# Graph attention on one core: 17 tiles of gathered rows in place of 10 fetched row by row from two DMA queues

## The chip, the core and the metric

One core of a Trainium2 chip. The metric is the device time of one execution in microseconds (us), lower is better; this document gives medians of several executions, and reads one profiled execution instruction by instruction. The engines are TensorE (PE), VectorE (DVE), ScalarE (ACT), GpSimd (POOL) and SyncE (SP). "SPq" and "ACTq" in the rows are the instruction streams of SyncE and ScalarE that issue DMAs.

## What is computed

A graph attention layer with 6250 nodes, 100000 edges sorted by target node, 96 features and 8 heads, then a residual and a layer norm. Cut to what matters:

```python
Q_h = (x @ Wq + bq); K_h = (x @ Wk + bk); V_h = (x @ Wv + bv)      # 6250 x 96
E   = edge_attr @ We + be                                          # 100000 x 96
score = K_h[src] * Q_h[dst] / sqrt(12) * E                         # per edge
score = exp(clip(score.sum over the 12 features of a head, -5, 5))
msg   = V_h[src] * score
h_out = segment_sum(msg, dst) / (segment_sum(score, dst) + 1e-6)
out   = layernorm(x + h_out)
```

## The kernel before

**Tables.** The node projections are made first (lines 444 to 460 on PE, copies on ACT), and written to two tables in device memory: `kv_table` (a row of 192 floats for each node, its K and V) and `q_table`. Then the edges are worked through.

**Groups.** Edges come in 99 groups, numbered `at` = 0 to 98: 96 of 8 tiles of 128 edges and three small ones (8, 4 and 2 tiles). For every group:

- POOL gathers the rows K and V of the edges' source nodes out of `kv_table` into `kv`, one indirect DMA for each tile (L424). For the first four groups it gathers rows of `x` instead (L422), and PE projects them. The buffer `kv` holds U = 8 groups, so group `at` waits for `msg_done` of group `at - 8`. From group CLOSE = 16 on, POOL also waits at the start of group `at` until `q_done` is at least `at - 1` (L410), which is when PE has finished the query product (L516) of group `at - 2`.
- SP loads, four groups ahead of the query product, the edge features (`ea`, L248), windows of the queries (`qwin`, L259) and the relative targets (`rel_table` into `q_parts`, L243). Iteration `at` of its loop waits for `q_done` of group `at` (L356). Every fourth iteration reads 8 window starts from memory into registers (`window_rows`, L253).
- PE, in its iteration `at`: if `at` is a multiple of 4, it turns the finished block of sums (L537); then it turns the edge products of group `at + 1` into rows (L527), multiplies the edge features of group `at + 2` (L506) and selects the queries of group `at + 2` (L516); last come the sums of group `at` (L576).
- DVE, in its iteration `at`: `qke` (L955, waits for the gather of the group), `qe` of group `at + 1` (L872), the sum over heads `logit` (L964), `clipped` (L970), `place` (L860), then the weights and `msg` (L979, L982), then the comparison `pick` for group `at + 3` (L851). Between these stand the steps 0 to 11 of the layer norm of the block before, at fixed places (`BLOCK_PLACES`): steps 0 to 4 in groups with `at % 4 == 0`, steps 5 and 6 with 1, steps 7 to 11 with 2. Step 7 (L908) waits for ACT.
- ACT, in its iteration `at`: if `at % 4 == 0` the copy `accT` of the sums (L684); the exponential of group `at` (L690); the copy of the edge product of group `at + 2` into `qe` (L676); for some groups the copy described next (L701); the single-row loads described next; and if `at % 4 == 1` the two steps of the layer norm's root, `spread` (L663, L665).

**Tiles by row.** In ten groups (`BY_ROW`) POOL leaves out the last of the 8 tiles. Its 128 rows are fetched one by one: `load_single_rows` reads source nodes from memory into registers (TENSOR_LOAD, L216) and issues one DMA of 768 bytes for each (L220) into `kv_rows`, which lies in the memory of `q_full` and so appears under that name in the rows. SP does this for five of the tiles, 8 rows in every iteration from 4 on, ACT for the other five, 8 rows in every iteration from 4 on. When a tile's 128 rows have landed, ACT copies it into `kv` (L701) in the iteration before its group.

All engines take their instructions in program order, so an activation that stands behind DMA issues in ACT's stream waits until they are issued. The order is written out by hand.

Of the kernel before, what the change touches and what calls it, by code (L numbers as in the profile page):

```python
# [4 lines left out]
P = 128  # L5
N = 6250
# [5 lines left out]
T = 8  # L12
# [5 lines left out]
NR = (NW + 1) * P  # L18
# [2 lines left out]
EPS_LN = 1e-5  # L21
U = 8
CLOSE = 2 * U
SP_ROWS, ACT_ROWS = 8, 8
SP_TURNS, ACT_TURNS = -(-P // SP_ROWS), -(-P // ACT_ROWS)
FROM = 4
SP_TILES = tuple(22 + SP_TURNS * i for i in range(5))
ACT_TILES = tuple(23 + ACT_TURNS * i for i in range(5))
BY_ROW = SP_TILES + ACT_TILES
XG = 4  # L30
TURNS = NB // U
KV_CHUNKS = (4, 6, 10, 10, 8, 6, 4, 2)
# [2 lines left out]
QB = 5  # L35
QW = 42
# [24 lines left out]
def lap(r, k, ring):  # L61

    return (U // ring) * r + k // ring + 1


def gnn_program(nc, xT, xrows, src, src_row, dst_group, dst_tile, eaT, w_node, w_edge, out):
    f32, bf16, i32 = mybir.dt.float32, mybir.dt.bfloat16, mybir.dt.int32
    ALU, ACT, AX = mybir.AluOpType, mybir.ActivationFunctionType, mybir.AxisListType

    kv_table = nc.dram_tensor("kv_table", (NR, 2 * D), f32, kind="Internal").ap()  # L70
# [6 lines left out]
    with ctx:  # L77
        def sb(name, shape, dt):
            return ctx.enter_context(nc.sbuf_tensor(name, shape, dt))
# [24 lines left out]
        identity = sb("identity", [P, P], f32)  # L104
        xg = sb("xg", [P, XG, T, D], f32)

# [13 lines left out]
        qbase_int = sb("qbase_int", [P, 2 * NG], i32)  # L120
# [9 lines left out]

        idx = sb("idx", [P, NG * T], i32)
        ea = sb("ea", [DA, EAR, GE], f32)
        row_id = sb("row_id", [1, len(BY_ROW) * P], i32)
        kv_rows = q_full[:].rearrange("p t d -> p (t d)").rearrange("p (i f) -> p i f", f=2 * D)[:, 0:len(BY_ROW)]
        qwin = sb("qwin", [P, QRING, 2, D], bf16)
        place = sb("place", [P, 2, T, PW], f32)
# [32 lines left out]
        q_full_up, q_hi, q_r, q_mid, q_up = sem("q_full_up"), sem("q_hi"), sem("q_r"), sem("q_mid"), sem("q_up")  # L169
# [4 lines left out]
        idx_in, idx_rest_in = sem("idx_in"), sem("idx_rest_in")  # L174
        xg_in = [sem(f"xg_in{i}") for i in range(XG)]
        turned, turned_up, conv_mm, conv_up = sem("turned"), sem("turned_up"), sem("conv_mm"), sem("conv_up")
        row_id_in, rows_up = sem("row_id_in"), sem("rows_up")
        rows_in = [sem(f"rows_in{i}") for i in range(len(BY_ROW))]
        kv_in = [sem(f"kv_in{i}") for i in range(U)]
# [28 lines left out]
        def alone(at, t):  # L208

            return at in BY_ROW and t == T - 1  # L210

        def load_single_rows(eng, i, j, rows):

            count = min(rows, P - j * rows)
            edge = i * P + j * rows
            nodes = nc.values_load_multi_w_load_instructions(  # L216
                row_id[0:1, edge:edge + count], engines=[eng.engine], min_val=0, max_val=N - 1,
                skip_runtime_bounds_check_because="source nodes of edges are nodes")[1]
            for p in range(count):
                eng.dma_start(kv_rows[j * rows + p:j * rows + p + 1, i], kv_table[bass.ds(nodes[p], 1), :]  # L220
                              ).then_inc(rows_in[i], 16)

        def engine_turns(eng, body, unrolled):
# [15 lines left out]
        def edge_pass(first):  # L239
# [11 lines left out]
            def window_rows(sp, g, count):  # L251

                return nc.values_load_multi_w_load_instructions(  # L253
                    qbase_int[0:1, bass.ds(2 * g, 2 * count)], engines=[sp.engine], min_val=0, max_val=NR - QW)[1]

            def load_windows(sp, slot, bases):

# [5 lines left out]
            with nc.Block() as block:  # L263

                @block.sync
                def _(sp):
                    if first:
                        sp.dma_start(idx[:, 0:XG * T], src[:, 0:XG * T]).then_inc(idx_in, 16)
                        sp.dma_start(wn[:], w_node).then_inc(w_in, 16)
# [19 lines left out]
                        for c in range(5, len(KV_CHUNKS)):  # L289
# [3 lines left out]
                                     ranges[:, 0:4].rearrange("g (m h) -> g m h", m=2)).then_inc(range_out, 16)  # L293
                        sp.dma_start(idx[:, XG * T:], src[:, XG * T:]).then_inc(idx_rest_in, 16)
                        sp.wait_ge(range_out, 16)
# [54 lines left out]
                    def loads(r, k, at):  # L350


                        if at >= NG:
                            return
                        g, j, q, half = U * r + k, at % BG, U // BG * r + k // BG, k // BG % 2
                        sp.wait_ge(q_done, g + 1)  # L356
                        sp.sem_inc(loads_begun, 1)
                        if j == 0 and at + QRING < NG:
                            ahead[:] = window_rows(sp, g + QRING, min(BG, NG - at - QRING))
                        if at + QRING < NG:  # L360
                            load_windows(sp, k % QRING, ahead[2 * j:2 * j + 2])
                        if at + EAR < NG:
                            load_ea(sp, g + EAR, k % EAR)
                        if at + RELR < NG:
                            load_rel(sp, g + RELR, k % RELR)
                        if not first:
                            return
                        if j == 0 and at < NB:
                            if at >= 2 * BG:
                                sp.wait_ge(block_steps, BLOCK_STEPS * q - 2 * BLOCK_STEPS + 4)  # L370
                                sp.sem_inc(stores_begun, 1)
                            load_rows(q, half)
                        if j == 1 and at >= 2 * BG:
                            store_rows(q - 2, half, at)
                        turn = at - FROM
                        if turn == 0:
                            sp.wait_ge(row_id_in, 16)
                            sp.wait_ge(kv_out, 16 * len(KV_CHUNKS))
                        if 0 <= turn < len(SP_TILES) * SP_TURNS:
                            load_single_rows(sp, turn // SP_TURNS, turn % SP_TURNS, SP_ROWS)  # L380

                    engine_turns(sp, loads, first)
                    if first:
# [14 lines left out]
                def _(pool):  # L398
# [6 lines left out]
                    def gathers(at):  # L405
# [5 lines left out]
                        if first and at == 0:  # L411
                            pool.wait_ge(idx_in, 16)
                        if first and at == XG:
                            pool.wait_ge(idx_rest_in, 16)
                            pool.wait_ge(kv_out, 16 * len(KV_CHUNKS))
                        k = at % U
                        for t in range(tiles(at)):
                            if first and alone(at, t):
                                continue
                            sources = bass.IndirectOffsetOnAxis(ap=idx[:, at * T + t:at * T + t + 1], axis=0)  # L420
                            if first and at < XG:
                                pool.indirect_dma_start(xg[:, k, t], None, xrows, sources).then_inc(xg_in[k], 16)  # L422
# [6 lines left out]
                    for s in range(U):  # L429
                        groups = len(range(s, NG, U)) - (1 if first and s < XG else 0)  # L430
                        missing = (T - TAIL_TILES[s]) if s < len(TAIL_TILES) else 0
                        missing += sum(1 for at in BY_ROW if first and at % U == s)
                        pool.wait_ge(kv_in[s], 16 * (T * groups - missing))
# [160 lines left out]
                def _(act):  # L594
# [84 lines left out]
                    def weights(r, k, at):  # L679

                        g = U * r + k
                        if first and BG <= at < NG and at % BG == 0:
                            act.wait_ge(sum_done, g)
                            nc.scalar.activation(accT[:, 1 - k // BG], psA[0:ML, 0:BW], ACT.Copy).then_inc(block_up, 1)  # L684
                        if at < NG:
                            act.wait_ge(clip_done, g + 1)
                            nt = tiles(at)
                            if at >= 2:
                                act.wait_ge(sum_done, g - 1)
                            nc.scalar.activation(msg[:, k % 2, 0:nt, D:ML],  # L690
                                                 clipped[:, k % 2, 0:nt * H].rearrange("p (t h) -> p t h", t=nt),
                                                 ACT.Exp).then_inc(wt_done, 1)


                        if at + 2 < NG:
                            edges_up(r, k + 2, at + 2)
                        if first and at + 1 in BY_ROW:
                            i = BY_ROW.index(at + 1)
                            act.wait_ge(rows_in[i], 16 * P)
                            act.wait_ge(msg_done, at + 1 - U + 1)  # L700
                            nc.scalar.activation(kv[:, (at + 1) % U, T - 1], kv_rows[:, i], ACT.Copy).then_inc(rows_up, 1)  # L701
                        turn = at - FROM
                        if first and turn == 0:
                            act.wait_ge(row_id_in, 16)
                            act.wait_ge(q_up, NR // P // QB)
                        if first and 0 <= turn < len(ACT_TILES) * ACT_TURNS:
                            load_single_rows(act, len(SP_TILES) + turn // ACT_TURNS, turn % ACT_TURNS, ACT_ROWS)
                        if first and BG <= at < NG and at % BG == 1:
                            block_rstd(U // BG * r + k // BG - 1, BC)
                    edges_up(0, 0, 0)  # L710
# [406 lines left out]
```

## Time and profile before

| | |
|---|---|
| median of 3 runs | 995.9 us (994.56 to 996.25) |
| profiled execution, its own time | 993.86 us |
| its span in the trace | 992.1 us |
| busy share of the span: POOL, DVE, PE, ACT | 74%, 66%, 65%, 19% |
| mean granted TensorE clock | 0.807 of full speed |
| indirect DMAs on POOL | 32 (L422) and 740 (L424) |
| single-row DMAs | 640 on SP, 640 on ACT |

The time of an execution lies about 1.8 us over its span. Busy time does not count the issuing of DMAs on SP and ACT, register work or waits: an engine with a low share can still have a full instruction stream. For POOL the gathers count as busy while their descriptors are made, and the short piece of time between two of them is put down to "issue".

### The profile page before, as it was taken

How to read it: one execution, taken by the hardware profiler on the slowest of the kernel's cores; microseconds unless marked ns; L12 is line 12 of the kernel's file. 1: busy time of each engine (PE TensorE's matmuls, PEld its weight loads, DVE VectorE, ACT ScalarE, POOL GpSimd, SP SyncE). 2: the span in 40 equal slices, each digit the busy share in tenths (PEclk: the TensorE clock that was granted, in tenths of full speed). 3: DMA queues.
4: the chain of work that ended last, by engine and by line, in shares of the span. 5: the costliest groups of instructions: out<-in, count | busy, mean ns of one | idle time of the engine just before them, and what ended most of it. 6: DMA issues, size and time to landing. Idle time of an engine off the chain costs nothing. (4 is left out here: it accounts for less than half of the span.)

```text
span 992.1 us, 15976 instructions
## 1 busy us (share of the span) xinstructions
PE 643.3 (65%) x3276; PEld 419.8 (42%) x3276; DVE 653.0 (66%) x1307; ACT 189.4 (19%) x378; POOL 737.3 (74%) x778
## 2 busy tenths in 40 slices
PE   6778777766566766666557656664675566657563
PEld 5655555444343434344334434443343344334342
DVE  6638987877666675766566656664775566657655
ACT  4842211111111111111111111111111111111111
POOL 7777777777777777777777777777777777777772
PEclk9888988788877777778777877788788878777876
DMA  6999776666655557656565665565665655664531
GB/s 201 311 285 241 185 188 184 188 173 172 176 147 168 150 140 185 165 138 175 143 173 150 164 177 149 139 177 145 168 170 145 180 147 137 177 176 123 145 80 47
DMA packets 103482, 165.77 MB, mean 167 GB/s; under 512 B 46285, under 2 KB 66126, under 8 KB 103375
## 3 DMA queue, kind: packets, MB, share of 16 engines
q1 hardware_dynamic: 64399, 84.88, 31.3%
q0 software_dynamic: 36544, 74.37, 28.4%
q10 hardware_dynamic: 2432, 5.41, 1.6%
q14 instruction: 79, 0.65, 0.2%
q8 instruction: 28, 0.46, 0.2%
HBM read 152.19 MB, written 12.39 MB: 166 GB/s over the span
## 5 line engine op out<-in xcount | busy, mean ns | idle before, releaser
L424 POOL DMA_INDIRECT kv<-kv_table,idx x740 | 703.7, 951 | 225.6 <-issue 224.3
L527 PE MATMUL psT<-identity,qe 96*128 96x96 f32 x782 | 115.3, 307 | 242.7 <-DVE qe L872 242.6
L955 DVE TENSOR_TENSOR qke<-psT,kv 128x768 f32<-128x768 f32 (+1 forms) x99 | 93.6, 945 | 266.5 <-DMA kv<-kv_table,idx 257.2
L506 PE MATMUL psE<-ea,we 97*96 97x512 f32 x392 | 259.7, 799 | 0.8 <-ACT kv L646 0.8
L527 PEld LDWEIGHTS psT<-identity,qe 96*128 96x128 f32 x782 | 93.2, 178 | 259.8 <-DVE qe L872 259.7
L576 PE MATMUL psA<-place,msg 128*104 128x104 f32 x1536 | 170.1, 266 | 22.4 <-DVE msg L982 22.1
L576 PEld LDWEIGHTS psA<-place,msg 128*104 128x104 f32 x1536 | 160.1, 180 | 51.2 <-DVE msg L982 45.0
L676 ACT ACTIVATE qe<-psE 96x1024 f32<-96x1024 f32 (+1 forms) x99 | 99.8, 1008 | 217.2 <-PE psE L506 217.2
L872 DVE TENSOR_TENSOR qe<-psQ,qe 96x1024 f32<-96x1024 f32 (+1 forms) x99 | 118.4, 1196 | 7.8 <-ACT qe L676 7.8
L506 PEld LDWEIGHTS psE<-ea,we 97*96 97x96 f32 x392 | 75.9, 219 | 80.2 <-issue 80.2
L690 ACT ACTIVATE msg<-clipped 128x64 f32<-128x64 f32 (+1 forms) x99 | 25.3, 255 | 419.8 <-DVE clipped L970 413.8
L860 DVE TENSOR_TENSOR place<-psI,rel_tile 128x832 f32<-128x832 f32 (+1 forms) x99 | 98.3, 993 | 0.0
L982 DVE TENSOR_TENSOR msg<-kv,psI 128x768 f32<-128x768 f32 (+1 forms) x99 | 93.4, 943 | 3.4
L964 DVE TENSOR_REDUCE logit<-qke 128x64 f32<-128x768 f32 (+1 forms) x99 | 91.4, 923 | 0.0
L516 PE MATMUL psQ<-q_parts,qwin 126*96 126x512 bf16 x196 | 70.6, 446 | 0.8 <-DVE q_parts L851 0.8
L516 PEld LDWEIGHTS psQ<-q_parts,qwin 126*96 126x96 bf16 x196 | 30.0, 153 | 83.2 <-issue 81.4
L851 DVE TENSOR_SCALAR q_parts<-q_parts,query_id 126x1024 bf16<-126x1024 bf16 x99 | 50.6, 511 | 14.7 <-DMA q_parts<-rel_table 14.7
L537 PE MATMUL psA<-identity,accT 104*128 104x104 f32 x73 | 15.8, 331 | 52.5 <-ACT accT L684 52.1
L422 POOL DMA_INDIRECT xg<-xrows,idx x32 | 33.1, 1034 | 11.1 <-issue 9.4
L537 PEld LDWEIGHTS psA<-identity,accT 104*128 104x128 f32 x73 | 10.5, 206 | 56.8 <-ACT accT L684 56.2
L970 DVE TENSOR_SCALAR clipped<-logit 128x64 f32<-128x64 f32 (+1 forms) x99 | 22.7, 230 | 4.4
L684 ACT ACTIVATE accT<-psA 104x384 f32<-104x384 f32 x24 | 11.8, 490 | 69.8 <-issue 63.3
(105 smaller groups left out, 349.5 us busy)
## 6 DMA issues: line engine op xcount, KB each, us to landing
ea<-eaT SPq DMA_DIRECT2D x99, 384.0 KB, 4.0
q_parts<-rel_table SPq DMA_DIRECT2D x99, 252.0 KB
kv<-kv_table,idx POOLq DMA_INDIRECT x740
q_full<-kv_table SPq DMA_DIRECT2D x640, 0.8 KB
q_full<-kv_table ACTq DMA_DIRECT2D x640, 0.8 KB
qwin<-q_table SPq DMA_DIRECT2D x198, 23.6 KB
xb<-xrows SPq DMA_DIRECT2D x24, 144.0 KB
out<-ob SPq DMA_DIRECT2D x24, 144.0 KB
```

The lines of the kernel that those rows point to most:

```text
L424: pool.indirect_dma_start(kv[:, k, t], None, kv_table, sources).then_inc(kv_in[k], 16)
L506: last = nc.tensor.matmul(psE[0:D, h, 0:size], we[:], ea[:, k % EAR, edge:edge + size], start=True, stop=True)
L516: last = nc.tensor.matmul(psQ[0:D, h, 0:size], qwin[0:QR, k % QRING, h], pick[0:QR, k % 2, h * GE // 2:h * GE // 2 + size], start=True, st ...
L527: last = nc.tensor.transpose(psT[:, t % 2, t // 2 * D:(t // 2 + 1) * D], qe[0:D, k % 2, t * P:(t + 1) * P], identity[0:D, 0:D])
L576: last = nc.tensor.matmul(sums[0:ML, off:off + PW], msg[:, s, t], place[:, s, t], start=opens, stop=closes)
L676: nc.scalar.activation(qe[0:D, k % 2, 0:edges], psE[0:D].rearrange("d b e -> d (b e)")[:, 0:edges], ACT.Copy).then_inc(e_up, 1)
L851: nc.vector.tensor_scalar(pick[0:QR, k % 2], rel[0:QR, k % RELR], query_id[0:QR], None, ALU.is_equal).then_inc(pick_done, 1)
L860: nc.vector.tensor_tensor(place[:, k % 2, 0:nt], ps_ids.unsqueeze(1).broadcast_to([P, nt, PW]), rel_tile[:, bass.ds(g * T, nt)].unsqueeze( ...
L872: nc.vector.tensor_tensor(qe[0:D, k % 2, 0:edges], psQ[0:D].rearrange("d b e -> d (b e)")[:, 0:edges], qe[0:D, k % 2, 0:edges], ALU.mult). ...
L955: nc.vector.tensor_tensor(qke[:, 0:nt].rearrange("p (t b) d -> p b t d", **by_bank), psT[:, :, 0:nt // 2 * D].rearrange("p b (t d) -> p b ...
L964: nc.vector.tensor_reduce(logit[:, 0:nt * H], qke[:, 0:nt].rearrange("p t (h d) -> p (t h) d", h=H), AX.X, ALU.add).then_inc(logit_done, 1)
L982: nc.vector.tensor_tensor(msg[:, s, 0:nt, 0:D].rearrange("p t (h d) -> p t h d", h=H), kv[:, k, 0:nt, D:2 * D].rearrange("p t (h d) -> p t ...
```

## The change

Seven more groups have a tile fetched by rows. ACT now fetches eleven tiles (groups 13, 21, ... 93), 16 rows in each iteration from 4 to 91, in two portions of 8: the first behind the exponential and ahead of the copy of `qe`, the second where the portion stood before. SP fetches six tiles (groups 18, 31, ... 83), 10 rows in each iteration from 4 to 81, in portions of 8 and 2. Each portion has its own read of source nodes from memory, and the host lays the node numbers out so that each portion begins at a multiple of 8. The eight window starts that SP reads in every fourth iteration are no longer asserted to lie in range.

```diff
-SP_ROWS, ACT_ROWS = 8, 8
+SP_ROWS, ACT_ROWS = 10, 16
+SP_STEP, ACT_STEP = 8, 8
 SP_TURNS, ACT_TURNS = -(-P // SP_ROWS), -(-P // ACT_ROWS)
 FROM = 4
-SP_TILES = tuple(22 + SP_TURNS * i for i in range(5))
-ACT_TILES = tuple(23 + ACT_TURNS * i for i in range(5))
+SP_TILES = tuple(18 + SP_TURNS * i for i in range(6))
+ACT_TILES = tuple(13 + ACT_TURNS * i for i in range(11))
...
-        def load_single_rows(eng, i, j, rows):
-
-            count = min(rows, P - j * rows)
-            edge = i * P + j * rows
+        def load_single_rows(eng, i, turn, rows, begin, end):
+
+            start = turn * rows + begin
+            count = min(turn * rows + end, P) - start
+            if count <= 0:
+                return
+            edge = row_slot(i, turn, rows, begin)
...
-                    qbase_int[0:1, bass.ds(2 * g, 2 * count)], engines=[sp.engine], min_val=0, max_val=NR - QW)[1]
+                    qbase_int[0:1, bass.ds(2 * g, 2 * count)], engines=[sp.engine], min_val=0, max_val=NR - QW,
+                    skip_runtime_bounds_check_because="the lowest target node of half a group, at most N")[1]
...
-                            load_single_rows(sp, turn // SP_TURNS, turn % SP_TURNS, SP_ROWS)
+                            for begin in range(0, SP_ROWS, SP_STEP):
+                                load_single_rows(sp, turn // SP_TURNS, turn % SP_TURNS, SP_ROWS, begin,
+                                                 min(SP_ROWS, begin + SP_STEP))
...
+                        turn = at - FROM
+                        rows_due = first and 0 <= turn < len(ACT_TILES) * ACT_TURNS
+                        if rows_due and turn == 0:
+                            act.wait_ge(row_id_in, 16)
+                            act.wait_ge(q_up, NR // P // QB)
+                        if rows_due:
+                            load_single_rows(act, len(SP_TILES) + turn // ACT_TURNS, turn % ACT_TURNS, ACT_ROWS,
+                                             0, ACT_STEP)
                         if at + 2 < NG:
                             edges_up(r, k + 2, at + 2)
...
-                        turn = at - FROM
-                        if first and turn == 0:
-                            act.wait_ge(row_id_in, 16)
-                            act.wait_ge(q_up, NR // P // QB)
-                        if first and 0 <= turn < len(ACT_TILES) * ACT_TURNS:
-                            load_single_rows(act, len(SP_TILES) + turn // ACT_TURNS, turn % ACT_TURNS, ACT_ROWS)
+                        if rows_due:
+                            load_single_rows(act, len(SP_TILES) + turn // ACT_TURNS, turn % ACT_TURNS, ACT_ROWS,
+                                             ACT_STEP, ACT_ROWS)
                         if first and BG <= at < NG and at % BG == 1:
                             block_rstd(U // BG * r + k // BG - 1, BC)
```

ACT's stream before, in iteration 5 and up to the exponential of iteration 6 (a pair "ISA, DMA" is one row fetched, and there are 8 pairs):

```order
L690 ACTIVATE msg<-clipped 128x8x8
L676 ACTIVATE qe<-psE 96x1024
L216 TENSOR_LOAD row_id
L220 ISA
L220 DMA q_full<-kv_table 1x192
...
L663 ACTIVATE spread<-spread 128x3
L665 ACTIVATE spread<-spread 128x3
L690 ACTIVATE msg<-clipped 128x8x8
```

The same stretch of ACT's stream after the change (lines have other numbers: 705 for 690, 691 for 676, 228 and 232 for 216 and 220, 678 and 680 for 663 and 665; there are 8 pairs in each portion):

```order
L705 ACTIVATE msg<-clipped 128x8x8
L228 TENSOR_LOAD row_id
L232 ISA
L232 DMA q_full<-kv_table 1x192
...
L691 ACTIVATE qe<-psE 96x1024
L228 TENSOR_LOAD row_id
L232 ISA
L232 DMA q_full<-kv_table 1x192
...
L678 ACTIVATE spread<-spread 128x3
L680 ACTIVATE spread<-spread 128x3
L705 ACTIVATE msg<-clipped 128x8x8
```

A read of node numbers and eight row DMAs now stand between the exponential and the copy of `qe`, and a second set stands where the first stood, ahead of `spread` and the next exponential.

SP's stream after the change, one iteration (two window loads, edge features, relative targets, then portions of 8 and of 2 rows; before, the second TENSOR_LOAD of `row_id` and two of the row DMAs were not there):

```order
L272 DMA qwin<-q_table 126x96
L260 DMA ea<-eaT 96x1024
L255 DMA q_parts<-rel_table 126x1024
L228 TENSOR_LOAD row_id
...
L228 TENSOR_LOAD row_id
L232 ISA
L232 DMA q_full<-kv_table 1x192
L232 ISA
L232 DMA q_full<-kv_table 1x192
L272 ISA
```

One TENSOR_LOAD and two pairs have come into SP's iteration. In every fourth iteration `window_rows` held one TENSOR_LOAD and 16 ISA instructions; now it is the TENSOR_LOAD alone.

POOL's stream, the gathers of groups, before and after in one piece of the difference:

```order
-L422 DMA xg<-xrows,idx 128x96 x32
-L424 DMA kv<-kv_table,idx 128x192 x740
+L437 DMA xg<-xrows,idx 128x96 x32
+L439 DMA kv<-kv_table,idx 128x192 x733
```

Seven gathers are gone.

## Rows read from the trace of the kernel before

**Rows 1.** Head of the page: span, busy time by engine.

```profile
span 992.1 us, 15976 instructions
PE 643.3 (65%) x3276; PEld 419.8 (42%) x3276; DVE 653.0 (66%) x1307; ACT 189.4 (19%) x378; POOL 737.3 (74%) x778
```

**Rows 2.** Groups: line, engine, operation, count | busy us, mean ns | idle before, releasers.

```profile
L424 POOL DMA_INDIRECT kv<-kv_table,idx x740 | 703.7, 951 | 225.6 <-issue 224.3 <-PE psQ L516 0.6 <-DVE msg L982 0.6
```

**Rows 3.** Timeline of POOL: start us, us, instruction [idle before <-releaser].

```profile
2.85 1.09 POOL L422 DMA_INDIRECT xg<-xrows,idx  x1 [1.70 <-DMA idx<-src]
...
165.52 0.95 POOL L424 DMA_INDIRECT kv<-kv_table,idx  x1 [0.30 <-issue]
166.77 0.94 POOL L424 DMA_INDIRECT kv<-kv_table,idx  x1 [0.30 <-issue]
...
973.73 0.95 POOL L424 DMA_INDIRECT kv<-kv_table,idx  x1 [0.30 <-issue]
```

**Rows 4.** Waits, whole span: total us, times, longest us.

```profile
DVE qke L955 <- DMA kv<-kv_table,idx: 257.2, 71, 7.9
ACT accT L684 <- issue: 63.3, 20, 3.5
ACT spread L663 <- issue: 62.8, 20, 3.4
DVE spread L908 <- ACT spread L665: 9.1, 6, 2.3
```

**Rows 5.** Groups (as in rows 2): the product that DVE makes from the `qe` copy.

```profile
L872 DVE TENSOR_TENSOR qe<-psQ,qe 96x1024 f32<-96x1024 f32 (+1 forms) x99 | 118.4, 1196 | 7.8 <-ACT qe L676 7.8
```

**Rows 6.** Timeline of ACT, iterations 4 to 12 in part, and 92.

```profile
100.50 0.26 ACT L690 ACTIVATE msg<-clipped 128x64 f32<-128x64 f32 x1 [1.29 <-DVE clipped L970]
...
109.86 3.29 ACTq L220 DMA_DIRECT2D q_full<-kv_table  x8
113.20 0.21 ACT L663 ACTIVATE spread<-spread 128x3 f32<-128x3 f32 x1 [3.21 <-issue]
113.44 0.21 ACT L665 ACTIVATE spread<-spread 128x3 f32<-128x3 f32 x1
115.26 0.26 ACT L690 ACTIVATE msg<-clipped 128x64 f32<-128x64 f32 x1 [1.62 <-DVE clipped L970]
...
127.44 0.49 ACT L684 ACTIVATE accT<-psA 104x384 f32<-104x384 f32 x1 [3.13 <-issue]
129.13 0.26 ACT L690 ACTIVATE msg<-clipped 128x64 f32<-128x64 f32 x1 [1.20 <-DVE clipped L970]
133.51 1.02 ACT L676 ACTIVATE qe<-psE 96x1024 f32<-96x1024 f32 x1 [4.12 <-PE psE L506]
134.39 3.20 ACTq L220 DMA_DIRECT2D q_full<-kv_table  x8
137.69 0.26 ACT L690 ACTIVATE msg<-clipped 128x64 f32<-128x64 f32 x1 [3.17 <-DVE clipped L970]
...
159.27 0.49 ACT L684 ACTIVATE accT<-psA 104x384 f32<-104x384 f32 x1 [3.12 <-issue]
160.77 0.26 ACT L690 ACTIVATE msg<-clipped 128x64 f32<-128x64 f32 x1 [1.01 <-DVE clipped L970]
...
933.21 0.26 ACT L690 ACTIVATE msg<-clipped 128x64 f32<-128x64 f32 x1 [6.90 <-DVE clipped L970]
```

**Rows 7.** Timeline of PE, the query product of group 14.

```profile
162.63 0.60 PE L516 MATMUL psQ<-q_parts,qwin 126*96 126x512 bf16 x2
```

**Rows 8.** Line L220 on ACT's queue: ns min/median/max.

```profile
L220 ACTq DMA_DIRECT2D q_full<-kv_table x640: 234/235/547, 103.2 to 849.3; - x160
```

**Rows 9.** Timeline of SP's stream, end of iteration 15, start of 16.

```profile
178.57 3.16 SPq L220 DMA_DIRECT2D q_full<-kv_table  x8
184.83 0.86 SPq L259 DMA_DIRECT2D qwin<-q_table  x2
```

More of the change, by code:

```diff
@@ L23 @@
 CLOSE = 2 * U
-SP_ROWS, ACT_ROWS = 8, 8
+SP_ROWS, ACT_ROWS = 10, 16
+SP_STEP, ACT_STEP = 8, 8
 SP_TURNS, ACT_TURNS = -(-P // SP_ROWS), -(-P // ACT_ROWS)
 FROM = 4
-SP_TILES = tuple(22 + SP_TURNS * i for i in range(5))
-ACT_TILES = tuple(23 + ACT_TURNS * i for i in range(5))
+SP_TILES = tuple(18 + SP_TURNS * i for i in range(6))
+ACT_TILES = tuple(13 + ACT_TURNS * i for i in range(11))
 BY_ROW = SP_TILES + ACT_TILES
+ROW_SLOTS = max(SP_TURNS * SP_ROWS, ACT_TURNS * ACT_ROWS) + 7 & ~7
 XG = 4
@@ L63, in lap, with row_slot @@
     return (U // ring) * r + k // ring + 1
+def row_slot(i, turn, rows, begin):
+    turns = -(-P // rows)
+    step = min(rows, SP_STEP if i < len(SP_TILES) else ACT_STEP)
+    return ROW_SLOTS * i + (step * turn if begin == 0 else step * turns + (rows - step) * turn)
 def gnn_program(nc, xT, xrows, src, src_row, dst_group, dst_tile, eaT, w_node, w_edge, out):
@@ L132, in gnn_program @@
         ea = sb("ea", [DA, EAR, GE], f32)
-        row_id = sb("row_id", [1, len(BY_ROW) * P], i32)
+        row_id = sb("row_id", [1, len(BY_ROW) * ROW_SLOTS], i32)
         kv_rows = q_full[:].rearrange("p t d -> p (t d)").rearrange("p (i f) -> p i f", f=2 * D)[:, 0:len(BY_ROW)]
@@ L219, in load_single_rows @@
             for p in range(count):
-                eng.dma_start(kv_rows[j * rows + p:j * rows + p + 1, i], kv_table[bass.ds(nodes[p], 1), :]
+                eng.dma_start(kv_rows[start + p:start + p + 1, i], kv_table[bass.ds(nodes[p], 1), :]
                               ).then_inc(rows_in[i], 16)
@@ L1098 @@
         first_edge += held
+    src_row = np.zeros((1, len(BY_ROW) * ROW_SLOTS), src.dtype)
+    for i, at in enumerate(BY_ROW):
+        rows, step = (SP_ROWS, SP_STEP) if at in SP_TILES else (ACT_ROWS, ACT_STEP)
+        for row in range(P):
+            begin = 0 if row % rows < step else step
+            slot = row_slot(i, row // rows, rows, begin) + row % rows - begin
+            src_row[0, slot] = src_pad[at, (T - 1) * P + row]
     arrays = {
@@ L1102 @@
         "src": np.ascontiguousarray(src_pad.reshape(NG * T, P).T),
-        "src_row": np.concatenate([src_pad[at, (T - 1) * P:T * P] for at in BY_ROW])[None],
+        "src_row": src_row,
         "dst_group": dst_pad,
```

## The prediction

> **What bounds the kernel now.** I read the busy times first, then the groups and waits, then the timeline engine by engine. POOL is busiest with 74% of the span [rows 1]. What matters is its gaps: of its 225.6 us idle at the gathers, 224.3 are "issue", the fixed piece between two gathers, and only 1.2 us are waits for others [rows 2]. The first gather starts at 2.85 and the 772nd and last at 973.73 [rows 3], so POOL works at one even pace of (973.73 - 2.85) / 771 = 1.259 us a gather, 10.0 us for a group of 8, and only some 17 us follow the last one's end. DVE waits 257.2 us in 71 places for gathered rows [rows 4]. So the end is set by POOL, wherever nobody holds POOL up.
>
> Two places need a closer look. At the start the consumers are late: by its pace POOL is done with the 40 gathers of groups 0 to 4 at about 2.85 + 40 x 1.26 = 53 [rows 3], and ACT's exponential of group 4 is at 100.50 [rows 6]. They catch up by running faster than POOL: the exponential of group 12 is at 160.77 [rows 6], (160.77 - 100.50) / 8 = 60.27 / 8 = 7.53 us a group against POOL's 10.0. Meanwhile POOL may not run ahead at will: from group 16 on it waits for the query product of group `at - 2`. In this trace that product (group 14, the 15th pair on L516) ends at 162.63 + 0.60 = 163.23, and POOL starts group 16 at 166.77, just behind one more gather of the group before, which starts at 165.52 [rows 3, 7]. **The gate is passed with 3.5 us to spare**, and nobody sees it in the list of waits.
>
> The second is ACT. Its busy share is 19% [rows 1], but DMA issues are not in it. `accT` waited 20 times for "issue" (63.3 us) and `spread` 20 times (62.8 us) [rows 4]: activations stand behind row DMAs and start the moment the last is issued. The stretch 109.86 + 3.29 = 113.15, `spread` at 113.20 shows it [rows 6].
>
> **The change, part by part.**
>
> *Seven gathers less on POOL:* 7 x 1.259 = 8.8 us less. All of it is on the path that ends the kernel, if the consumers keep up. One of them is in group 13, so POOL is ready for group 16 at about 166.77 - 1.25 = 165.52.
>
> *Twice as many rows on ACT.* One portion costs the read of node numbers, about 0.88 us (`qe` at 133.51, first row DMA at 134.39), and eight issues, 3.20 to 3.29 us in the rows shown; I take 3.25, and 0.05 to the next activation, together 4.18 [rows 6]. The portion in front of the `qe` copy has no row of its own, I take the same price. It falls into time in which ACT waited for PE's edge product (4.12 us in iteration 8, [rows 6]; in most iterations near 1 us), so it isn't simply added. What counts is how long ACT's stream becomes while it is catching up:
>
> - An ordinary iteration: two portions, 8.36, and 0.1 until the exponential (134.39 + 3.20 = 137.59, exponential at 137.69): 8.46 us. DVE's work from the `qe` copy, which ends 4.18 + 1.02 = 5.2 us into the iteration, is the product of 1.2 us [rows 5] and the 1.6 us from there to the next exponential (next point), together 8.0, so ACT's stream leads.
> - `at % 4 == 1`: the two `spread` steps come behind the second portion (0.24 + 0.21), DVE's step 7 waits for them, and the next exponential comes 1.61 us after them (113.65 to 115.26 [rows 6]): 8.36 + 0.45 + 1.55 = 10.36 us. DVE waits for this now already, 9.1 us in six places [rows 4].
> - `at % 4 == 3`: `accT` comes behind the second portion and the exponential 1.69 (127.44 to 129.13) or 1.50 us later (159.27 to 160.77) [rows 6]: 8.36 + 1.6 = 9.96 us.
>
> Four iterations take 8.46 + 10.36 + 8.46 + 9.96 = 37.2 us, 9.3 each, where two times four took 60.27. The exponential of group 4 stands ahead of the first portion and stays at 100.50; that of group 12 comes at 100.50 + 74.5 = 175.0 in place of 160.77, and the query product of group 14 ends 2.46 us behind it as now (163.23 - 160.77), at 177.4.
>
> *The gate.* POOL is ready at 165.5 and is let through at 177.4: **a wait of 11.9 us that does not exist now**. Everything behind it on POOL's stream moves. It should happen once: counted from the exponential of group 12, the products of groups 15, 16, 17 and 18 are there after some 11, 19, 30 and 40 us (the exponentials of 13 to 16 come after 8.5, 18.8, 27.3 and 37.2, and each product at most some 2.5 behind), and POOL gets to the gates of groups 17 to 20 after 12.5, 22.5, 31.4 and 41.4. Then the consumers, at 9.3 a group, are faster than POOL, which needs 10.0 and in groups with a tile by row 8.8, 9.8 on average; what lag is left is worked off at half a us a group.
>
> *SP's rows, two more in an iteration:* 2 x 0.40 (3.16 / 8) [rows 9] and a second read, about 0.9 as on ACT, 1.7 us. Iteration 16's loads begin at 184.83 though its release came long before, 3.1 us after the last row issue at 181.73; nothing but `window_rows` stands there [rows 9]. Without assertions it should take 0.9 too, a saving of about 2.2 in every fourth iteration. SP keeps up with the consumers' 7.53 us in this stretch, so it needs at most 7.53 + 1.7 - 0.55 = 8.7, less than ACT's 9.3, and it loads four groups ahead. I cost it at nothing. If SP came over 9.8 a group it would starve PE.
>
> *Copies of seven more tiles on ACT*, of 0.35 us or so each, lie beside the read of node numbers: nothing.
>
> **The sum.** 992.1 - 8.8 + 11.9 = 995.2 for the span of the profiled execution, 3.1 more than its 992.1, and with the 1.8 around it 997.0 for 993.86. The median of the runs, 995.9, is 2.0 over that execution. On the median: 995.9 + 3.1 = **999.0 us**, 0.3% slower. Bounds of this case: if the waits at `spread` and `accT` are hidden, eight iterations of 8.4 give 167.7, the product at 170.1 and a wait of 4.6, a net of -4.2 (991.7). If every issue took longer, since ACT's row DMAs have a maximum of 547 ns against a median of 235 [rows 8], with 3.5 a portion each iteration is 0.5 longer, 8 of them 4 us, a net of +7 (1003). The case's own range is 996 to 1003.
>
> The trace has 3.2 us of stream time for eight 768-byte loads on ACT [rows 6], 0.40 each. The Trainium skill ("DMA: Bandwidth & Descriptors", section "Issuing engines are not separate DMA queues") says that issuing from several engines only saves sequencer time, which is usually small beside the DMA itself. By this rule the doubled issues would cost next to nothing, no gate would close, and the sum would be 987.1; the trace disagrees with it for DMAs this small.
>
> **Rivals.**
>
> *Faster, the gate stays open (987.1 us, 0.17; partly closed, 988 to 995, 0.13).* The mechanism: the portion ahead of the `qe` copy fills time in which ACT is idle anyway and the consumers go on at 7.5 to 8 us a group. The gate keeps open as long as group 14's product comes before 165.5, that is up to 2.3 us late, or 0.28 us an iteration. For it: ACT is idle over half of the catch-up, and DVE's and PE's own chain is what sets 7.53 now. Against it: two portions alone are 8.36 us by rows. It gives 995.9 - 8.8 = 987.1.
>
> *ACT becomes the bound over the whole length (slower still, 0.18).* With c us an iteration the exponential of group 92 comes at 100.5 + 88 c; by POOL's pace with my wait it comes at 933.21 - 8.8 + 11.9 = 936.3 [rows 6]. ACT overtakes at c = 9.50, and each 0.1 above costs 8.8 us. For it: I stand only 0.2 below; the `qe` copy of a slow edge product (4.12 us, [rows 6]) waits past my first portion, and the two streams issue at the same time, which the maximum of 547 ns may show. Against: most portions take 3.2. With c = 9.6 it gives 1008.
>
> *The change does its part and a tile's rows come late.* SP's first tile is fetched up to iteration 16 and copied in 17, with one iteration to spare where there were two; ACT would wait at the copy. A late landing of 2 us in each of 17 tiles would be worked off by the consumers' slack; within the first case.
>
> **How the numbers follow.** The gate closes by about 12 us: 0.52; gate open or partly: 0.30; ACT bound: 0.18. Two tenths of a per cent, about what can be told here, are 2 us. Faster than 993.9: nearly all of the open cases, 0.29. Slower than 997.9: the ACT-bound case, and about seven in ten of the first, 0.54. Same: 0.17. The single value is the first case's, 999.0. Since the open gate and the far end of the ACT-bound case hold more than 2 in 10 together, the range takes in 987.1 and reaches to 1004.
>
> **What would show it.** In the changed kernel: the list of waits has POOL <- PE psQ (the query product) with one wait of about 12 us near 165 to 177; gaps of exponentials over iterations 4 to 12 of about 8.5, 10.4, 8.5, 10.0; 765 gathers at an unchanged 1.25 us; DVE waiting for gathers less than 257.2, and only from about the middle of the span on; `accT` and `spread` still behind "issue" in nearly every case. Wrong it is if ACT's iteration is below 8 us, if POOL shows no wait at group 16, or if DVE never waits for gathers late in the span, which means ACT bounds.

## The result, and the profile after

The changed kernel takes 1002.68 us (median of 4 runs, 1002.53 to 1004.57) where the kernel before took 996.08 (4 runs, 994.56 to 996.28): 6.6 us more, a ratio of 1.0073 with a 95% interval of 1.006 to 1.0085. It is slower, as forecast, by twice the 3.1 us that were forecast. The two traces are further apart than the medians: the span grew by 1002.8 - 992.1 = 10.7 us, since the profiled execution of the kernel before (993.86 us) lies 2.2 under its median and that of the changed kernel 1.9 over its own.

The head of the page of the changed kernel; its profiled execution is the longest of the four, 1004.57 us (span 1002.8):

```profile
span 1002.8 us, 18441 instructions
PE 673.4 (67%) x3276; PEld 436.4 (44%) x3276; DVE 657.4 (66%) x1307; ACT 192.2 (19%) x385; POOL 733.3 (73%) x771
POOL 7777774577777777777777777777777777777772
```

The line of slices has a dent that answers to nothing before: in the seventh and eighth of 40, from about 150 to 200 us, POOL is at 40% and 50% and not at 70%. The timeline of POOL there, and its last gather:

```profile
181.96 0.95 POOL L439 DMA_INDIRECT kv<-kv_table,idx  x1 [16.46 <-PE psQ L531]
...
984.12 0.95 POOL L439 DMA_INDIRECT kv<-kv_table,idx  x1 [0.30 <-issue]
```

This is the first gather of group 16. It waited 16.46 - 0.30 = 16.2 us for PE's query product, the one thing that the rows of before [rows 3] don't have. The last gather starts at 984.12 in place of 973.73. The account: 973.73 - 8.8 for seven gathers + 16.2 = 981.1; the other 3.0 us are POOL's pace, (984.12 - 2.81 - 16.2) / 764 = 1.263 us a gather against 1.259. That pace belongs to this execution and is not shown to be the change's: with ACT's part alone, which has the same wait, and without the gate it is 1.260, and over all traces here it goes from 1.257 to 1.263. The other three executions of the changed kernel have spans of 1000.3 to 1000.8, some 2 us shorter; what they waited at the gate has no trace.

What POOL waited for at 16, in PE's timeline (edge product and query product of group 14):

```profile
176.52 1.21 PE L542 MATMUL psT<-identity,qe 96*128 96x96 f32 x8
177.52 3.23 PE L521 MATMUL psE<-ea,we 97*96 97x512 f32 x4
180.59 0.60 PE L531 MATMUL psQ<-q_parts,qwin 126*96 126x512 bf16 x2
```

And why it is late, in the timeline of ACT (the exponentials of groups 4 and 12, and one iteration between):

```profile
101.82 0.26 ACT L705 ACTIVATE msg<-clipped 128x64 f32<-128x64 f32 x1 [1.29 <-DVE clipped L990]
...
130.47 3.20 ACTq L232 DMA_DIRECT2D q_full<-kv_table  x8
133.77 1.02 ACT L691 ACTIVATE qe<-psE 96x1024 f32<-96x1024 f32 x1 [3.96 <-issue]
134.94 3.20 ACTq L232 DMA_DIRECT2D q_full<-kv_table  x8
138.19 0.49 ACT L699 ACTIVATE accT<-psA 104x384 f32<-104x384 f32 x1 [3.40 <-issue]
139.72 0.26 ACT L705 ACTIVATE msg<-clipped 128x64 f32<-128x64 f32 x1 [1.04 <-DVE clipped L990]
...
177.04 0.26 ACT L705 ACTIVATE msg<-clipped 128x64 f32<-128x64 f32 x1 [1.00 <-DVE clipped L990]
```

From group 4 to 12 the consumers took 177.04 - 101.82 = 75.2 us, 9.4 a group, where they took 60.3 [rows 6]. ACT was hardly ever idle by its own choice: `qe` and `accT` start when the last row DMA in front of them is issued. The waits of the whole span:

```profile
ACT qe L691 <- issue: 258.2, 64, 4.4
DVE qe L892 <- ACT qe L691: 98.9, 59, 3.5
ACT accT L699 <- issue: 70.4, 22, 3.4
ACT spread L678 <- issue: 70.3, 22, 3.5
DVE qke L975 <- DMA kv<-kv_table,idx: 60.1, 21, 5.5
DVE spread L928 <- ACT spread L680: 44.7, 20, 2.7
DVE qke L975 <- ACT kv L724: 36.2, 16, 3.7
POOL kv L439 <- PE psQ L531: 21.3, 17, 16.5
```

DVE, which waited 257.2 us for gathers [rows 4], waits 60.1: it now waits for ACT instead, in places that were at 7.8 [rows 5] and 9.1 [rows 4].

### The profile page after: what moved, and what is told of

Read it like the earlier page. It is cut to its first block and busy times, and to the rows that moved or that the text cites. A ratio compares the mean times of both kernels' runs of the same rounds, so it can differ in the third digit from the quotient of the medians.

```text
span 1002.8 us, 18441 instructions
## 1 busy us (share of the span) xinstructions
PE 673.4 (67%) x3276; PEld 436.4 (44%) x3276; DVE 657.4 (66%) x1307; ACT 192.2 (19%) x385; POOL 733.3 (73%) x771
## 5 line engine op out<-in xcount | busy, mean ns | idle before, releaser
L521 PE MATMUL psE<-ea,we 97*96 97x512 f32 x392 | 276.3, 845 | 0.8 <-ACT kv L661 0.8
L591 PE MATMUL psA<-place,msg 128*104 128x104 f32 x1536 | 181.8, 278 | 36.0 <-DVE msg L1002 35.6
L591 PEld LDWEIGHTS psA<-place,msg 128*104 128x104 f32 x1536 | 170.4, 190 | 69.1 <-DVE msg L1002 64.2
L975 DVE TENSOR_TENSOR qke<-psT,kv 128x768 f32<-128x768 f32 (+1 forms) x99 | 93.1, 940 | 100.6 <-DMA kv<-kv_table,idx 60.1
L521 PEld LDWEIGHTS psE<-ea,we 97*96 97x96 f32 x392 | 79.7, 229 | 86.0 <-issue 86.0
L552 PE MATMUL psA<-identity,accT 104*128 104x104 f32 x73 | 18.4, 382 | 104.6 <-ACT accT L699 104.1
L928 DVE TENSOR_TENSOR spread<-spread 128x3 f32<-128x3 f32 (+1 forms) x25 | 4.0, 162 | 47.0 <-ACT spread L680 44.7
L906 DVE TENSOR_SCALAR rzb<-psA 128x24 f32<-128x24 f32 (+1 forms) x25 | 4.5, 181 | 44.3 <-PE psA L552 44.3
```

The source lines that it names most:

```text
L521: last = nc.tensor.matmul(psE[0:D, h, 0:size], we[:], ea[:, k % EAR, edge:edge + size], start=True, stop=True)
L591: last = nc.tensor.matmul(sums[0:ML, off:off + PW], msg[:, s, t], place[:, s, t], start=opens, stop=closes)
L975: nc.vector.tensor_tensor(qke[:, 0:nt].rearrange("p (t b) d -> p b t d", **by_bank), psT[:, :, 0:nt // 2 * D].rearrange("p b (t d) -> p b ...
```

## The experiments

The experiments ran on two chips, in three groups, each with its own runs of the kernel before (993.26, 995.60 and 993.95 us); times are compared with those, and an expectation in us, counted from another time of the kernel before, is best read as a ratio.

**Which engine's part.** SP's part alone (with the missing assertions; ACT's eight rows stand behind the copies, as before), and ACT's part alone:

```diff
-SP_ROWS, ACT_ROWS = 10, 16
+SP_ROWS, ACT_ROWS = 10, 8
-ACT_TILES = tuple(13 + ACT_TURNS * i for i in range(11))
+ACT_TILES = tuple(23 + ACT_TURNS * i for i in range(5))
...
```

> SyncE's part of the change and the missing assertions alone: SP fetches six tiles, 10 rows an iteration; ACT fetches five tiles, 8 rows an iteration, where the portion stood before. 11 tiles by row, one gather less than before. Both theories: the ACT stream is untouched, the gate at group 16 stays open, 996.1 - 1.26 = 994.8 us. If SP's longer iteration is what hurts, it is above 997.

992.22 us against 993.26 before, ratio 0.999 (0.9981 to 0.9999): 1.0 us less, where one gather fewer is worth 1.26, and no harm to be seen in SP's longer iteration.

```diff
-SP_ROWS, ACT_ROWS = 10, 16
+SP_ROWS, ACT_ROWS = 8, 16
-SP_TILES = tuple(18 + SP_TURNS * i for i in range(6))
+SP_TILES = tuple(22 + SP_TURNS * i for i in range(5))
```

> ScalarE's part alone: ACT fetches eleven tiles, 16 rows an iteration in two portions, SP five tiles as before, 8 rows an iteration. 16 tiles by row. Both theories: the loss is in ACT's stream, so a wait of POOL at group 16 of 14 to 17 us and 1002 to 1004 us. If the loss came from SP's stream or from two streams together it would be under 998.

1000.47 us against 993.26, ratio 1.0076 (1.0062 to 1.0091), the same as the whole change, and the same wait in POOL's timeline:

```profile
181.49 0.94 POOL L439 DMA_INDIRECT kv<-kv_table,idx  x1 [16.53 <-PE psQ L531]
```

The loss is all in ACT's part, which has six gathers fewer and not seven. The assertions alone:

```diff
-                    ..., min_val=0, max_val=NR - QW)[1]
+                    ..., min_val=0, max_val=NR - QW,
+                    skip_runtime_bounds_check_because="the lowest target node of half a group, at most N")[1]
```

> The kernel before with the assertions on the eight window starts taken away and nothing else. SP is released by the consumers and is not on the path that ends the kernel, so no change: 1.000 of the kernel before, within 0.001. If SP's stream paced the start, where it never waits, the catch-up would be faster but POOL, which sets the end, would not: the same.

993.4 us against 993.95, ratio 0.9998 (0.9989 to 1.0007): nothing.

**Is the gate the loss, or ACT's pace?** The changed kernel without POOL's wait for query products:

```diff
-CLOSE = 2 * U
+CLOSE = 4 * NG
```

> The changed kernel with GpSimd's wait for the query products taken away (it still waits for msg_done of eight groups before). Theory A, the wait at group 16 is the whole loss: POOL is no longer held for 16 us, the end comes some 15 us earlier, about 987 us, 9 us under the kernel before. Theory B, ScalarE's stream is a bound of its own: the exponential of group 4 comes at about 101.8 and 88 iterations of 9.55 us (the mean of iterations 4 to 64 of the changed kernel's trace) bring that of group 92 to about 942, where it was at 944.7, so the end comes only 1 to 3 us earlier, about 1000 to 1001.5, and DVE hardly waits for gathers before group 85.

986.79 us against 993.26, ratio 0.9934 (0.9921 to 0.9947). The change is turned from a loss of 0.7% into a gain of 0.7%. It looks like theory A's number, but by luck: theory A had it 9 us under the kernel before, and it is 6.5 under, since the kernel before is 2.8 us faster on this chip. And theory B's mechanism is in the trace as well; the exponentials of groups 92, 96 and 98 there:

```profile
937.93 0.26 ACT L705 ACTIVATE msg<-clipped 128x64 f32<-128x64 f32 x1 [1.21 <-DVE clipped L990]
...
964.78 0.26 ACT L705 ACTIVATE msg<-clipped 128x64 f32<-128x64 f32 x1 [1.00 <-DVE clipped L990]
...
972.04 0.21 ACT L705 ACTIVATE msg<-clipped 128x16 f32<-128x16 f32 x1 [1.80 <-DVE clipped L990]
```

Group 92 comes at 937.93: the first exponential with rows behind it was at 98.42 here, so 88 iterations took 9.54 us each, just as theory B had it, and DVE never waited for a gather: the list of waits has no such line. What theory B missed is the tail. After iteration 91 ACT has no rows to issue, and the last gathers of groups 94 to 98 start 4 to 12 us before DVE comes to them, so groups 93 to 96 take (964.78 - 937.93) / 4 = 6.7 us each. In the changed kernel the exponential of group 92 is at 944.68 and that of 98 at 989.30, 44.6 us further, since there the last groups still come at POOL's pace; here it is 34.1. So **without the gate ACT's stream bounds nearly the whole length, and most of the backlog is paid back in the last seven groups**. Most, since the last exponential starts 7.0 us after the last gather (965.04) and not 5.2 as in the changed kernel.

The control, the kernel before with the same edit:

> The kernel before with the same wait taken away, as a control. Both theories: POOL passes that gate freely in the kernel before (3.5 us to spare at group 16), so nothing changes, 996 us within 1 us. If the wait also kept POOL from making descriptors too early and so did some good, this would be slower.

995.64 us against 993.26, ratio 1.0022 (1.0012 to 1.0031), 2.4 us more. The spans don't show it: 991.8 us in the profiled execution, 989.5 to 992.1 in all, like those of the kernel before on that chip (989.8 to 993.8). The execution's own time lies 3.7 to 5.2 us over its span where it lies 1.6 to 2.9 over it in every run of the other kernels. The gate does no good inside the span; why the rest is longer stays open.

The gate looser by one group:

```diff
-                            pool.wait_ge(q_done, at - 1)
+                            pool.wait_ge(q_done, at - 2)
```

> The changed kernel with POOL's gate looser by one group: it waits for the query product of group at - 3. That of group 13 ended at 170.7 in the changed kernel's trace and at 167.1 in that of ACT's part alone, where POOL is ready at 165.5 to 165.8, so the wait at group 16 falls from 16.2 to 2 to 6 us. The end comes 10 to 13 us earlier as far as POOL sets it: 987 to 991 us. If the wait were only a symptom and ACT's pace set the end, above 996.

993.54 us against 995.60, ratio 0.9981 (0.997 to 0.9993). POOL's wait there:

```profile
171.28 0.94 POOL L439 DMA_INDIRECT kv<-kv_table,idx  x1 [6.07 <-PE psQ L531]
```

The wait shrank from 16.2 to 5.8 us and the time with it, from a ratio of 1.0073 to 0.9981. The 987 to 991 expected were counted on a chip where the kernel before takes 993.3; the ratio would make it 991.4 there, just past the upper end. POOL waited at two later gates as well, by 1.2 and 0.9 us. DVE waited once, 2.7 us, for a gather in this trace: here too ACT's pace sets most of the length.

**Is it the length of ACT's stream, and where?** Both portions behind the copies:

```diff
-                        if rows_due:
-                            load_single_rows(act, ..., 0, ACT_STEP)
                         if at + 2 < NG:
                             edges_up(r, k + 2, at + 2)
...
+                        if rows_due:
+                            load_single_rows(act, ..., 0, ACT_STEP)
                         if rows_due:
                             load_single_rows(act, ..., ACT_STEP, ACT_ROWS)
```

> The changed kernel with both ACT portions behind the copies, none ahead; 17 tiles by row. By the length of ACT's stream (two portions of 4.18 us wherever they stand) ordinary iterations stay at 8.4 to 8.6, the wait at group 16 stays at 13 to 17 us and the time at 999 to 1001 us, up to 2 us less because DVE no longer waits for the tile's copy in 16 groups. If the place of the front portion is what holds PE and DVE up, the wait at group 16 falls under 8 us and the time under 994.

1112.67 us against 995.60, ratio 1.1185 (1.1169 to 1.1201). Both expectations missed by more than 100 us, and not in the direction that either named. ACT's timeline from the copy of iteration 23 to the exponential of group 25:

```profile
306.63 1.02 ACT L691 ACTIVATE qe<-psE 96x1024 f32<-96x1024 f32 x1 [1.70 <-PE psE L521]
307.51 8.18 ACTq L232 DMA_DIRECT2D q_full<-kv_table  x16
315.73 0.49 ACT L699 ACTIVATE accT<-psA 104x384 f32<-104x384 f32 x1 [8.09 <-issue]
317.43 0.26 ACT L705 ACTIVATE msg<-clipped 128x64 f32<-128x64 f32 x1 [1.20 <-DVE clipped L990]
321.64 1.02 ACT L691 ACTIVATE qe<-psE 96x1024 f32<-96x1024 f32 x1 [3.96 <-PE psE L521]
322.52 7.43 ACTq L232 DMA_DIRECT2D q_full<-kv_table  x16
330.06 0.26 ACT L705 ACTIVATE msg<-clipped 128x64 f32<-128x64 f32 x1 [7.40 <-issue]
```

And in the waits of the whole span:

```profile
ACT msg L705 <- issue: 331.6, 46, 7.9
```

`accT` stands behind 16 rows and waits 8.1 us for their issues; PE's turn of the block and the edge products behind it start late with it, and the `qe` copy has to wait 4 us for them with nothing to issue in between. Then come 7.4 us of rows, and the exponential of group 25 behind them. In the changed kernel the exponentials waited for issues only once, 1.2 us; here 46 times. The exponentials of groups 24, 25, 26, 27 and 28 lie at 317.43, 330.06, 340.60, 349.40 and 361.15: 43.7 us for four, 10.9 each, above POOL's pace, with POOL waiting 130.2 us in 33 places for query products. **A portion costs far less ahead of the copy than behind it: ahead, it fills the wait for PE; behind, the next exponential waits for it**. A bare sum of ACT's stream hides that.

Twelve rows an iteration, 8 ahead and 4 behind:

```diff
-SP_ROWS, ACT_ROWS = 10, 16
+SP_ROWS, ACT_ROWS = 10, 12
-ACT_TILES = tuple(13 + ACT_TURNS * i for i in range(11))
+ACT_TILES = tuple(16 + ACT_TURNS * i for i in range(8))
```

> Two thirds of ACT's part: 12 rows an iteration, 8 ahead of the copy and 4 behind, eight ACT tiles and SP's six, 14 tiles by row. ACT's stream is 4.18 + 2.5 + 0.1 = 6.8 us, shorter than the 7.5 that the other engines need, so an ordinary iteration takes 7.3 to 7.6 and one with a wait for spread or accT 8.6 to 9.0: about 8.1 on average, the product of group 14 comes at 100 + 8 x 8.1 + 3 = 168 and POOL waits 1 to 4 us. Four gathers less give 5.0 us: 990 to 992 us where the kernel before takes 993.3. If the price goes with the rows, two thirds of the loss: 5 us of net loss, 998.

994.92 us against 995.60, ratio 0.9992 (0.9979 to 1.0004), the single times from 990.68 to 999.5. Neither number, and not decided: the profiled execution is one of the long ones (998.91), and in it POOL waited 7.4 us at group 16:

```profile
174.19 0.94 POOL L439 DMA_INDIRECT kv<-kv_table,idx  x1 [7.73 <-issue]
```

The list calls it "issue", but the product of group 14 ended at 172.26 + 0.85 = 173.11 just before. Its exponentials of groups 4 and 12 are at 103.18 and 168.96, 8.2 us a group as expected; it is the start that is 3 us late. Since the exponential of group 4 lies anywhere from 98.4 to 103.2 us in the profiles of the kernels here, and a closed gate hands such a lateness on, the wide spread would follow; this is not shown, since the other executions have no trace.

**A better version.** ACT doubles its rows only from iteration 20, when the consumers have caught up:

```diff
+EIGHT_UNTIL = 20
-ACT_TILES = tuple(13 + ACT_TURNS * i for i in range(11))
+ACT_TILES = tuple(21 + ACT_TURNS * i for i in range(10))
...
-                        turn = at - FROM
+                        turn = (at - FROM) // 2 if at < EIGHT_UNTIL else at - EIGHT_UNTIL + (EIGHT_UNTIL - FROM) // 2
+                        behind_only = at < EIGHT_UNTIL
```

> The changed kernel with the gate in place, but ACT fetches 8 rows an iteration behind its copy, as before, in iterations 4 to 19, and 16 rows in two portions only from iteration 20, when the consumers have caught up; ten ACT tiles in place of eleven, 16 tiles by row in all. If the loss comes from ACT's longer stream during the catch-up, the gate at group 16 stays open (POOL waits under 1 us), the six tiles more by row than before give 6 x 1.26 = 7.5 us, and the time is 0.9925 of the kernel before, about 985.7. If ACT at 9.54 us an iteration over 72 iterations were the bound in any case, the exponential of group 92 would still come at 224 + 72 x 9.54 = 911, ahead of POOL, so the same. If the longer stream costs wherever it stands, about 996 to 1000.

987.85 us against 995.60, ratio 0.993 (0.9918 to 0.9943). POOL at group 16, and the waits:

```profile
166.11 0.94 POOL L440 DMA_INDIRECT kv<-kv_table,idx  x1 [0.37 <-issue]
```

```profile
DVE qke L978 <- DMA kv<-kv_table,idx: 171.7, 56, 6.6
POOL kv L440 <- PE psQ L532: 1.5, 5, 0.3
```

POOL passes into group 16 with the usual 0.3 us or so between two gathers, its waits for PE come to 1.5 us in the whole span, and its last gather starts at 965.47. Here the same 16 rows an iteration on ACT cost nothing that shows: 7.7 us less, where six gathers are worth 7.5. With SP at 12 rows an iteration on top:

```diff
-SP_ROWS, ACT_ROWS = 10, 16
+SP_ROWS, ACT_ROWS = 12, 16
-SP_TILES = tuple(18 + SP_TURNS * i for i in range(6))
+SP_TILES = tuple(16 + SP_TURNS * i for i in range(7))
```

> The late doubling of e5_double_late (ACT 8 rows an iteration to iteration 19, 16 from there) with SP fetching 12 rows an iteration in portions of 8 and 4, seven SP tiles and ten ACT tiles: 17 tiles by row, as many as the change, with POOL's gate in place. SP's iteration is about 8.5 us with 10 rows in the trace of e5_double_late and would be 9.3 with 12, ACT's is 9.54, both below POOL's mean of 9.8. If only the catch-up was the trouble, the gate stays open and seven gathers fewer give 8.8 us: 0.9912 of the kernel before. If SP at 9.3 us an iteration holds up the catch-up (7.5 us an iteration before), its loads, which run four groups ahead, are late by group 12 to 16, POOL waits at group 16 for more than 5 us, and the time is above 0.996.

985.36 us against 993.95, ratio 0.9915 (0.9902 to 0.9929). 17 tiles by row, as many as in the change, and 8.6 us less, all that seven gathers are worth. The list of waits of this kernel has a warning in it that turned out harmless:

```profile
DVE qke L978 <- ACT kv L726: 48.5, 16, 13.0
ACT kv L726 <- DMA q_full<-kv_table: 12.8, 2, 9.3
POOL kv L440 <- PE psQ L532: 1.2, 4, 0.3
```

SP's first tile came late and held DVE up for 13 us at group 16. POOL wasn't touched: its waits for PE come to 1.2 us in the whole span. The consumers made the 13 us good.

## Why the prediction was right, and where its size was off

- **Direction and mechanism held.** Seven gathers less, a catch-up slowed by ACT's stream, one wait of POOL at group 16 for the query product of group 14: each is in the trace. That the loss comes from ACT's rows during the catch-up is shown from three sides: ACT's part alone gives it, opening the gate removes it, and the same rows from iteration 20 on don't give it. That the median lay within the range, near its upper end, owes something to luck: the profiled span grew by 10.7 us, not 3.1.
- **The term that was mis-sized is the wait at the gate,** 16.2 us for 11.9 in the trace. By its own steps: the exponential of group 4 came at 101.82 and not 100.50 (+1.3, the start of that execution); eight iterations took 75.2 for 74.5 (+0.7); the product ended 181.19 - 177.04 = 4.15 us behind the exponential of group 12 and not 2.46 (+1.7); POOL started 0.77 us behind the product, which I had at nothing, and was ready 0.28 later than I had it. Together 4.2. The 1.7 is PE's clock: turns and edge product took 1.21 + 3.23 us, and 0.82 + 1.88 before. The edge product before, then the stretch from 97 to 178 us before and after:

```profile
160.91 1.88 PE L506 MATMUL psE<-ea,we 97*96 97x512 f32 x4
...
97.00:178.00 81.00, 61.82 (x348) 40.50 (x348) 68.29 (x139) 16.82 (x32) 61.21 (x65) 0.87 0.71 186
...
97.00:178.00 81.00, 56.81 (x284) 36.91 (x283) 56.87 (x111) 13.79 (x25) 52.03 (x55) 0.78 0.61 163
```

  In such a row stand the busy times of PE, PEld, DVE, ACT and POOL and then the granted clock: 0.87 of full speed before and 0.78 after the change, each a mean over stretches at either level (2.4 and 1.2 GHz). PE was less busy in the slower catch-up and got less of its clock, but that the one made the other, and with it the 1.7, is not shown. With SP's part alone the catch-up was as fast as before (7.57 us a group) and the mean clock the same 0.87, and still the edge product took 3.05 us and the query product came 4.04 us behind the exponential. Which level the clock had just then counts.
- **The range:** the case's own range was put at 996 to 1003 though its lower bound had been worked out as 991.7; nothing hung on it in the end.
- **ACT's iteration was priced well where nothing else was in it:** 8.4 to 8.7, 10.3 to 10.9, 8.4 to 8.7 and 9.9 to 10.7 us in iterations 4 to 63 of the trace against 8.46, 10.36, 8.46 and 9.96, a mean of 9.44 against 9.3.
- **The copies of tiles at nothing were wrong.** On ACT's stream they are free, but DVE waits for them, 36.2 us in 16 places; an iteration with `at % 4 == 0` and such a copy takes 9.1 to 9.5 us in place of 8.4 to 8.7. With them the mean from group 4 to 64 is (674.99 - 101.82) / 60 = 9.55, not 9.3, just past the 9.50 that I gave as the point from which ACT bounds. The lag is not worked off by half a us a group: DVE waits for gathers only from about group 66 on, not from the middle.
- **The rival of ACT as the bound** is there to a part. Its price of 8.8 us for each 0.1 was too simple, since the last seven groups give a backlog back, as the kernel without the gate shows. In the changed kernel it was close: by POOL's path with the measured wait the exponential of group 92 would come at 933.21 - 8.8 + 16.2 = 940.6, by ACT's pace at 101.82 + 88 x 9.54 = 941.3. It came at 944.68, and DVE waited for gathers just before it, so POOL set the end.
- **The rival of the open gate:** the portion ahead of the copy does fill idle time, as that rival had it, and more than I thought (its removal to the back costs 110 us). But two portions are 8.4 us of stream all the same. The Trainium skill ("DMA: Bandwidth & Descriptors", section "Issuing engines are not separate DMA queues") says that the time to initiate a DMA is usually small relative to the DMA itself. The prediction says that the trace disagrees, and that goes too far: for a single load the traces bear the page out. A row takes 0.40 us of the stream; in the last kernel above SP issued the last rows of its first tile by 189.71, and the copy that waited for them started at 191.44, 1.7 us later. What fails is to conclude from this that many issues cost next to nothing: eight of them take 3.2 us of ACT's stream, one after the other.
- **SP** cost nothing that shows, as forecast, and the assertions neither.

## What to carry to other kernels

An engine that issues DMAs has a stream whose length its busy share doesn't show; add it up as issues times their price, and put issues where the engine waits anyway. Before loading a stream, look for the stretch in which its slack is smallest: here it was the catch-up after the start, iterations 4 to 16 of 99, and a semaphore gate that is passed with 3.5 us to spare shows in no list of waits. A lag that is caught up costs little or nothing (13 us at one group here); a gate that turns a lag into a stop of the bounding engine makes it a loss (16.2 us here).

## What was not expected of the hardware

- PE's granted clock was 0.78 in place of 0.87 in the stretch in which its work was merely spread out. Six of the nine edge products there took 2.8 to 3.6 us in place of 1.88, three of eleven before. The traces of the kernels with ACT's 16 rows from the start have 0.78 to 0.87 in this stretch, all others 0.87 to 0.96; the cause stays open.
- The time of an execution over its span isn't fixed: 1.6 to 2.9 us in the other kernels here, 3.7 to 5.2 in the kernel before with the gate taken out, with a span that did not change.
